# The feed-forward part of a two-layer transformer pipeline, run one step later

## The reference, cut to what matters

```python
def _layer(x, wqkv, qs, ksc, wo, lg, lb, w1, b1, w2, b2):
    h = shift_token(x)                      # second half of the features: from the token before
    q, k, v = heads(h @ wqkv)               # 8 heads of 64
    q = l2norm(q) * qs
    k = l2norm(k) * ksc
    q, k = rotary_xpos(q, k)
    x = x + local_attention(q, k, v) @ wo   # windows of 64
    h = shift_token(x)
    mu = h.mean(-1); var = h.var(-1)
    h = (h - mu) / jnp.sqrt(var + 1e-05) * lg + lb
    a, g = jnp.split(h @ w1 + b1, 2, axis=-1)
    return x + (a * gelu(g)) @ w2 + b2      # hidden width 341
```

## Time and profile before

| | |
|---|---|
| median of 3 runs | 2002.58 us (2001.6 to 2005.05) |
| profiled execution, its own time | 2002.01 us |
| its span, from the first to the last instruction | 1999.7 us |
| mean granted TensorE clock | 0.925 of full speed |
| PE busy | 1648.4 us, 82% of the span |
| DVE busy | 1364.6 us, 68% |
| ACT busy | 1185.8 us, 59% |
| POOL busy | 1087.2 us, 54% |

### The profile page before, as it was taken

How to read it: one execution, slowest core, us unless ns; L and a number is a source line. 1 busy time by engine, 2 the same in 40 slices (tenths; PEclk the granted TensorE clock), 3 DMA queues, 4 the chain that set the end, 5 groups by cost and what they waited for, 6 DMA issues and landing times. The chain is left out here.

```text
span 1999.7 us, 47702 instructions
## 1 busy us (share of the span) xinstructions
PE 1648.4 (82%) x18737; PEld 1206.3 (60%) x18737; DVE 1364.6 (68%) x2187; ACT 1185.8 (59%) x1958; POOL 1087.2 (54%) x632
## 2 busy tenths in 40 slices
PE   1389997899999348999999649899889889999963
PEld 1356665566666215777767437777777767777752
DVE  3378885555445509999999557877777777777633
ACT  0166676344444116777777528777777777777752
POOL 0176663344444206767677567666666666666412
PEclk9999999999999668999999869999999999999986
DMA  3100000000000030000000101111111111111101
GB/s 101 47 2 2 3 2 9 13 7 7 12 6 0 8 86 2 2 2 2 3 2 2 59 22 23 26 30 23 22 23 23 24 27 23 23 23 23 26 20 42
DMA packets 52354, 40.22 MB, mean 20 GB/s; under 512 B 24424, under 2 KB 44172, under 8 KB 52020
## 3 DMA queue, kind: packets, MB, share of 16 engines
q1 hardware_dynamic: 52148, 37.35, 7.3%
HBM read 15.75 MB, written 2.13 MB: 9 GB/s over the span
## 5 line engine op out<-in xcount | busy, mean ns | idle before, releaser
L438 POOL TENSOR_TENSOR a_prob<-a_prob,a_top 128x1024 f32<-128x1024 f32 x192 | 359.6, 1894 | 132.7 <-DVE a_top L651 132.7
L645 DVE TENSOR_TENSOR a_prob<-ps,a_table 128x1024 f32<-128x1024 f32 x192 | 226.1, 1219 | 110.1 <-PE ps L505 55.0
L877 POOL TENSOR_TENSOR e_hh<-e_h,e_hh 128x512 fp32r<-128x512 f32 x112 | 144.1, 1290 | 194.9 <-ACT e_hh L864 193.2
L612 ACT ACTIVATE a_probT<-ps 128x1024 f32<-128x1024 f32 x192 | 196.3, 1022 | 89.0 <-PE ps L515 89.0
L651 DVE TENSOR_REDUCE a_top<-a_prob 128x4 f32<-128x1024 f32 (+1 forms) x192 | 225.2, 1214 | 9.1 <-issue 0.4
L515 PEld LDWEIGHTS ps<-ident,a_prob 128*128 128x128 f32 x1536 | 167.0, 141 | 95.2 <-issue 59.4
L607 ACT ACTIVATE a_prob<-a_prob 128x1024 f32<-128x1024 f32 x192 | 202.3, 1054 | 32.8 <-POOL a_prob L438 32.8
L515 PE MATMUL ps<-ident,a_prob 128*128 128x128 f32 x1536 | 207.7, 278 | 8.5 <-ACT a_probT L612 3.4
L1136 POOL TENSOR_TENSOR i_qk<-i_qk,i_rn 128x1024 f32<-128x1024 f32 x64 | 121.7, 1903 | 119.3 <-DVE i_rn L1460 119.2
L1123 POOL TENSOR_TENSOR i_qk<-i_raw,i_rot 128x1024 f32<-128x1024 f32 x64 | 152.7, 2385 | 58.9 <-ACT i_raw L1343 58.9
L898 DVE TENSOR_TENSOR e_h<-ps,e_sg 128x512 f32<-128x512 f32 x112 | 77.4, 691 | 143.1 <-PE ps L764 117.8
(11 more groups left out here) (211 smaller groups left out, 3867.5 us busy)
## 6 DMA issues: line engine op xcount, KB each, us to landing
i_V<-i_V SPq DMA_DIRECT2D x96, 130.0 KB, 2.3
a_prob<-skew_scratch SPq DMA_DIRECT2D x2, 2048.0 KB, 9.3
X<-in_L_attn_x SPq DMA_DIRECT2D x4, 512.0 KB, 6.0
a_table<-in_c_l_table SPq DMA_DIRECT2D x1, 2048.0 KB, 7.7
e_xs<-Y SPq DMA_DIRECT2D x8, 256.0 KB, 2.3
i_ms<-Y SPq DMA_DIRECT2D x16, 128.0 KB
out_dram<-X SPq DMA_DIRECT2D x4, 512.0 KB, 3.2
i_ms<-Y SPq DMA_DIRECT2D x16, 127.0 KB
```

What stands on the lines that cost most here:

```text
L438: nc.gpsimd.tensor_tensor(s, s, top[:, slot].unsqueeze(2).broadcast_to([P, HG, KW]), ALU.subtract).then_inc(shifted, 1)
L612: nc.scalar.activation(probT[:, n % 4].rearrange("p (b n) -> p b n", b=2), ps[:, 4:6, :], ACT.Copy).then_inc(pT_sb, 1)
L645: nc.vector.tensor_tensor(prob[:, slot].rearrange("p (b x) k -> p b x k", b=2), ps[:, 2 * (n % 2):2 * (n % 2) + 2, :].rearrange("p b (x k) ...
L877: nc.gpsimd.tensor_tensor(hh[0:n, b % HBUF, 1, :], h[0:n, b % HBUF, :], hh[0:n, b % HBUF, 0, :].bitcast(F32), ALU.subtract).then_inc(h_lo, 1)
```

## The change

Every phase of the feed-forward part from `deviations` on moves by one step: `deviations`, `mlp_tokens` and `keep_mlp_tokens` from `ahead` 7 to 8, the chunks from 8 to 9, `gelu` and `gate` from 11 to 12, `mlp_out` from 12 to 13. `moments` moves from 6 to 7 and now stands between `quotient` and `keep_value` on DVE. `inverse_deviation` stays at 7 but moves to the end of ACT's step. `deviations` now runs at the head of DVE's step, behind `norms`, and `square_sums` of that step moves to its end, behind `keep_mlp_tokens`. The normalised tokens lie in `mT` instead of `G`.

```diff
-        mn = G[:, 0, :].rearrange("p (k e) -> p k e", k=4)
+        mn = mT[:].rearrange("p (k e) -> p k e", k=4)
...
 (ACT)
             for step in range(FIRST, LAST):
-                R, c = round_at(step, 11)
+                R, c = round_at(step, 12)
                 if R is not None and c == 0:
                     gelu(R)
...
-                R, c = round_at(step, 7)
-                if R is not None and c == 0:
-                    inverse_deviation(R)
                 if is_tile(step):
                     exp(step)
...
-                R, c = round_at(step, 8)
+                R, c = round_at(step, 9)
                 if R is not None and c < NC:
                     keep_gate(R, c)
+                R, c = round_at(step, 7)
+                if R is not None and c == 0:
+                    inverse_deviation(R)
...
 (DVE)
             def deviations(R):
                 dve.wait_ge(m_seed, R + 1)
-                after(dve, hm_done, R)
+                after(dve, ga_ps, R * NC)
...
                 if not odd and is_tile(step + 2):
                     norms(e)
-                if is_tile(step + LEAD - 1):
+                M, c = round_at(step, 8)
+                normal = M is not None and c == 0
+                if normal:
+                    deviations(M)
+                elif is_tile(step + LEAD - 1):
                     square_sums(step + LEAD - 1)
...
                 if is_tile(step - 1):
                     quotient(step - 1)
                 R, c = round_at(step, 7)
                 if R is not None and c == 0:
-                    deviations(R)
-                    keep_mlp_tokens(R)
-                R, c = round_at(step, 8)
+                    moments(R)
+                R, c = round_at(step, 9)
                 if R is not None and c < NC:
                     keep_value(R, c)
-                R, c = round_at(step, 6)
-                if R is not None and c == 0:
-                    moments(R)
+                if normal:
+                    keep_mlp_tokens(M)
+                    if is_tile(step + LEAD - 1):
+                        square_sums(step + LEAD - 1)
                 dve.drain()
```

More of the change, by code:

```diff
@@ L998, in inner_layers @@
         block = c.enter_context(nc.Block())
-        FIRST, LAST = -(LEAD + 1), TT + 10
+        FIRST, LAST = -(LEAD + 1), TT + 11
         NLOAD = DEPTH * (1 + 1 + 3 + 4 + 2 + 2)
@@ L1028, in banks_01_free @@
             projections_taken(eng, step - 1)
-            R, c = round_at(step - 1, 8)
+            R, c = round_at(step - 1, 9)
             if R is not None and c < NC:
@@ L1032, in banks_01_free @@
                 eng.wait_ge(a_sb, R * NC + c + 1)
-            R, c = round_at(step - 1, 7)
+            R, c = round_at(step - 1, 8)
             if R is not None and c == 0:
@@ L1040, in bank_3_free @@
             after(eng, y_att, min(step - 2, TT))
-            R, c = round_at(step - 1, 12)
+            R, c = round_at(step - 1, 13)
             if R is not None and c < 2:
@@ L1303, in _ @@
                     project_out(step - 2)
-                R, c = round_at(step, 12)
+                R, c = round_at(step, 13)
                 if R is not None and c < 2:
@@ L1316, in _ @@
                     mlp_chunk(R, c)
-                R, c = round_at(step, 7)
+                R, c = round_at(step, 8)
                 if R is not None and c == 0:
@@ L1553, in keep_mlp_tokens @@
                 dve.wait_ge(m_T, R + 1)
-                after(dve, ga_ps, R * NC)
                 nc.vector.tensor_scalar(mT[:, :], ps[:, 0, :], vecs[:, l, 0:1], vecs[:, l, 1:2], ALU.mult, ALU.add).then_inc(m_sb, 1)
```

## The result

| | before | after |
|---|---|---|
| median of 4 runs, us | 2002.84 (2001.6 to 2005.05) | 2020.88 (2018.87 to 2028.45) |
| profiled execution: time, span, us | 2002.01, 1999.7 | 2020.66, 2018.4 |
| granted clock of the span | 0.925 | 0.933 |

The ratio is 1.0096, with the 95% interval [1.0068, 1.0123]: the changed kernel is slower by 18 us, where 1986 was forecast and 1974 to 2016 given as range. (In the changed kernel `keep_mlp_tokens` has line L1554, `keep_value` L1560; the others are as before.)

The account below looks back on a forecast made before the run. PE's order of work was taken as the bound, with its stalls and slow clock to gain. Steps of 9.5 + 12.6 + 13.4 + 11.0 = 46.5 against 47.77 us give -15 over 12 periods, edges -1: 1986 us, range 1974 to 2016.

Parts of the forecast that it names:

- the layout of type 0: Loaded step with `gelu`, `gate`, `deviations`, `mlp_tokens`: late mask gives PE a new 2.7 us stall; step 12.6 us with clock loss.
- rival 1: Type 0: POOL's `gate` blocks the fourth L1547, delaying mask and PE: about +2.2 us a period, 2013 us; chance 0.35.
- its worse half: Type 0: L1144 slips in too before the fourth L1547: +15 us more, 2028 us; left out of the range.
- The second stall chain: Type 1: `keep_mlp_tokens`, `square_sums`, `squares`, `keep_qkT`, next `square_sums` and mask add make PE wait 1.8 us in all.
- Its clock term: Type 1: the clock may fall after two short gaps; half of 1.5 us was taken, 0.7 us.
- The clock term of type 0: Type 0: clock falls in the 2.7 us gap, costing 1.5 us; a small overlap then took 13.2 to 12.6.
- Moments at nothing, types 2 and 3: Type 3 hides `moments` (about 1.6 us) in DVE's wait for the last chunk, 9.5 us; type 2 takes 11.0.
- Rival 3: Type 0: `project_out` or the exponentials wait for ACT beyond the mask: 1 us a period, 1998 us; chance 0.05.
- The edges: Tail before last `stage` about -5 us; round 14's `gelu`, `gate`, `mlp_out` after round 15's DMA about +4; together -1.

Follow-up runs that it names:

- e1: Changed kernel with POOL's `gate` moved behind the `rotate` of its step: 1978.57 us, ratio 0.9871 to the kernel before.
- e2: Changed kernel with an accumulator output added to each L1547, for times alone: 1979.41 us, ratio 0.9886 to the kernel before.
- e4: Changed kernel with the loaded step's `square_sums` moved to between `sines` and `bank_3_written`: 1996.63 us, ratio 0.9970 to the kernel before.
- e7: Changed kernel with deviations ahead of `norms` on DVE and the loaded step's `square_sums` before `bank_3_written`: 1950.36 us, ratio 0.9733 to the kernel before.
- e3: Changed kernel with deviations ahead of the step's `norms` on DVE: 1964.28 us, ratio 0.9794 to the kernel before.
- e6: Changed kernel with `rotate` before `gate`, and `moments` back at the end of the type 2 step: 2006.09 us, ratio 1.0017 to the kernel before.
- e5: Changed kernel with `gate`'s halves swapped, 85x512 before 128x1024: 2058.35 us, ratio 1.0278 to the kernel before.
- e9: Changed kernel with `gate` as three instructions, 128x512, 128x512, 85x512: 1998.34 us, ratio 0.9980 to the kernel before.
- e11: Changed kernel with `gate` as three instructions, 85x512, 128x512, 128x512: 1997.46 us, one run.

## Why the prediction was wrong

- **The failed step** is the layout of type 0: "They continue at 3.7; as before, L1547 starts 0.55 us behind the blocked one's end, at 4.25 and ends at 5.4." Start and block of L1540 were right (4.34 and 1.83 us measured); that L1547 runs through unblocked was not. It is held by `gate`, as rival 1 says, and the mask add starts at 7.40 instead of 5.4: 2.0 us a step. Rival 1 charged 2.2, though its own times (7.3 in place of 5.4) give 1.9. e1 and e2 show the cause from both sides.
- **The reason for the wrong choice** stood in the text: whether the fourth L1547 comes before `gate` "hangs on 0.1 us of my arithmetic". The spacing of 0.26 us and `gate` at 4.9 were both right within 0.1 us (0.26 and 4.93 measured), and by them the fourth, at 5.03, already starts after `gate`. Nothing in that sum spoke against the rival; the doubt was only whether such an instruction can be blocked, and on that the row pair of the earlier trace rows leant the right way.
- **Beyond rival 1**: in its worse half it let L1144 in too. What stood in the long steps was L1144 and L1123 behind it, 3.60 us, and which of the two happened hung on whether the third or the fourth L1547 met L1143. It happened twice, not each time, so +6.8 us. Rival 1 at its own 1.9 a period gives 47.7 without the clock loss in type 1 (46.5 + 1.9 - 0.7); the typical one was 47.74.
- **The second stall chain** (type 1, 1.8 us) was right in its place and size: 12.70 us against 10.85 + 1.8 = 12.65. e4 takes it away. Its clock term was not: the granted clock stayed at 1.00, and the 0.7 us goes. "Half of 1.5" was a mean of two cases, of which the run showed one.
- **The clock term of type 0** was forecast at 1.5 us each time, less 0.6 for an overlap that no row shows (13.2 became 12.6), so 0.9. In the changed kernel that holds: PE's busy time is 9.85 us there and 8.82 in e7's fast step, 1.0 less. In e1, e3 and e7 it comes in some steps only, at the same waits.
- **A wait that the prediction does not have** is the 0.54 us at L1179 in type 0. `inverse_norm` of the odd step now stands ahead of the last `keep_gate` on ACT. The wait lies in front of the one for the mask and shortens it by as much, so here it costs nothing.
- **Moments at nothing, types 2 and 3**: right. 11.06 for 11.0, and 9.51 for 9.5; e6 shows what the old place would have cost.
- **Rival 3** was hidden in the changed kernel behind the longer mask stall and came out in e3 and e7, at 1.05 us where 1.0 was charged.
- **The edges** were put at -1 together and came to +11.7 from step 57 on. Before the last moments -5 was forecast and -2.1 came. Behind them +4 was forecast and +5.8 came. The one that was missed is step 60, 17.56 us: I had counted periods to step 59 and let the last loaded steps be like the others, but there `gate` has `normalise` right behind it. It makes nearly all of the +8.0 of steps 57 to 60, out of 18.7 us, and in e1 it stays where all the other steps are mended.
- **What the earlier trace rows say, two SBUF inputs are blocked, held for every run**: no such instruction of the pipeline that started within a POOL instruction ran free. The Trainium skill (SBUF — State Buffer, "Who interferes with whom") gives more than the rows of before could: that `tensor_scalar` in a two-port mode excludes GpSimd as well. The runs now bear out that L1547 is held, with 2.37 us for the one that `gate`'s first half holds, 0.34 for one that nothing holds, and 0.40 for the form with an accumulator. (The mode that it runs in shows in no trace.) That sentence of the prediction had the right sign, and I gave it 0.35 where the arithmetic beside it left no room for another outcome.

## What to carry to other kernels

When an instruction of VectorE moves, lay POOL's instructions of the new place beside it and ask of each pair that could overlap whether this form is held; if the answer hangs on 0.1 us, take the held case as the forecast, and look at the ends of the loop, where the queues have other neighbours. Order on POOL or DVE alone, with the same instructions, was worth from 1950 to 2058 us here (e7 and e5). If one VectorE chain releases a POOL instruction, put what POOL would hold ahead of what releases it (e3).

## What was unexpected of the hardware

- A TENSOR_SCALAR of 128x128 f32 from SBUF to SBUF that runs in 0.34 us takes up to 6.00 us beside POOL (e5); its form with an accumulator takes 0.40 us, with 0.08 more for reading the accumulator, and is not held (e2).
- A held VectorE instruction is let in between two POOL instructions, or not. L1547 was when the next one was of 85x512 or 128x512, and was not when it was of 128x1024; the two-input L1540 was let in ahead of 128x1024 too. The open question is what decides; e5, e9 and e11 differ in nothing but this order and split.
- A few nanoseconds decide between a step of 14.5 and one of 17.9 us: `gate` began 0.577 to 0.629 us behind the first L1547 in the ten common steps, and 0.574 and 0.575 in the two long ones.
- The granted clock after waits of 0.5, 1.0 and 1.0 us is full in one step and 0.87 in the next with the same instructions and waits (11.43 and 12.91 us).
